# Routing of an AdaLN mixture-of-experts layer block by block instead of by pairs of blocks, with the square roots on GpSimd

## The chip, the cores and the metric

One NeuronCore of one Trainium2 chip runs the whole kernel in one launch. The metric is the device time of that launch in microseconds (us), the median of several runs; less is better. The engines are TensorE (PE, with PEld for its weight loads), VectorE (DVE), ScalarE (ACT), GpSimd (POOL) and SyncE (SP), which here only issues DMAs.

## The reference

4096 tokens (128 samples of 32) of width 256. Each sample's tokens are first mixed with a 32x32 matrix picked by the sample's condition; the result goes through a feed-forward layer with one shared part and 32 routed experts in 4 groups. Each token takes the two best groups and, in these, the eight best experts.

```
xc = einsum('bct,bcd->bdt', x, weights[conditions])
scores = sigmoid(xc @ gate_w.T)
sb = scores + gate_bias                      # (T, 32), four groups of 8
group_scores = top_k(sb by group, 2).sum()   # the best 2 of 4 groups
topi = top_k(sb of the chosen groups, 8)
w = scores[topi]; w = w / w.sum() * 2.5      # the combine weights cw
x_lat = xc @ fc1_w.T                         # width 128
h = relu(x_lat @ w1[e].T)**2 * cw[e]
routed = (sum_e h @ w2[e].T) @ fc2_w.T
shared = relu(xc @ shared_up_w.T)**2 @ shared_down_w.T
out = x + shared + routed
```

## The kernel before

The program is written by hand for each engine: five instruction lists, each executed in its own order, tied by semaphores. Nothing reorders them.

**First stage.** The tokens are 8 blocks of 512. For block b, TensorE makes `project(b)` (the condition mix, 16 matmuls), `gate_and_latent(b)` (24 matmuls, `t_banks`), and two `shared_up` units of 12 matmuls of 512 columns and two `shared_down` units of 24 matmuls of 256 columns (units 2b and 2b+1). ScalarE rounds and squares, VectorE makes the low halves (`rest`, `rest_of_projection`: every matmul is done in three terms of a high and a low part), and adds the shared result to x (`add_shared`, L946), which SP stores.

**Routing**, also in the first stage, is done on VectorE for a batch of two blocks (1024 tokens, `NB` = 8 tiles of 128 tokens, `BATCHES` = 4): `group_scores`, `pick_groups`, `largest`, `mark`, `combine_weights`. TensorE's `rank(k)` (L548 to L560) counts how many earlier tokens chose each group; VectorE reads it (`read_rank`, L1079) and makes the row index of each token in `slot_of_token`. The weight enters an expert under a square, so its square root is stored: ScalarE's `root_of_weights` (L794, a Sqrt, which needs another activation table than Sigmoid) and four VectorE operations (L1061 to L1072, a reciprocal and one Newton correction) write it into `payload`. GpSimd's `scatter(k)` (L463) then writes 16 row tiles of batch k to DRAM (`rows_dram`), two indirect DMAs for each tile of 128 tokens.

When all is counted, VectorE makes `tile_table`; SP waits for it (`table_ready`), writes four pads (L386), reads the table's entries into registers, loads the first experts' weights (L371, 8 DMAs of 512 KB), and waits for all scatters (L400) before it loads the sorted rows (`sid_sb` L359, `rows_sb` L352).

**Second stage.** 19 tiles of 512 sorted rows go through the four pairs of experts of their group, and GpSimd adds the results to the output with 76 indirect DMAs (L486). It begins on TensorE with `transpose_s(0)` (L621), which needs `sid_sb`; behind it in TensorE's list stand the last two `shared_down` units.

The experts' weights are split into high and low parts in the first stage too, group by group: SP loads the raw weights (`load_raw`, L274) only when the previous group's are split, ScalarE rounds (`round_weights`, L801), VectorE subtracts (`rest_of_weights`, L952), SP stores (`store_split`, L321).

## Time and profile before

| | |
|---|---|
| median of 3 runs | 497.52 us (496.77 to 497.75) |
| the profiled execution's own time | 494.15 us |
| its span, first to last instruction | 492.1 us |
| first stage, up to the first transpose of the second | 208.9 us |
| busy in the span: PE, DVE, ACT, POOL | 423.7, 308.4, 275.1, 204.7 us |
| instructions on POOL | 158 |
| mean granted TensorE clock | 0.927 of 2.4 GHz |

An engine's busy time says how much work it had, and not whether anything waited for it. In this kernel the first stage has gaps on every engine, and its end is set by whichever of several chains is last; the rows below are therefore mostly timelines, which give for each instruction its start, its duration and, in brackets, how long its engine had been idle and what released it.

### The profile page before, as it was taken

How to read it: one execution, taken by the hardware profiler on the slowest of the kernel's cores; microseconds unless marked ns; L12 is line 12 of the kernel's file. 1: busy time of each engine (PE TensorE's matmuls, PEld its weight loads, DVE VectorE, ACT ScalarE, POOL GpSimd, SP SyncE). 2: the span in 40 equal slices, each digit the busy share in tenths (PEclk: the TensorE clock that was granted, in tenths of full speed). 3: DMA queues.
4: the chain of work that ended last, by engine and by line, in shares of the span. 5: the costliest groups of instructions: out<-in, count | busy, mean ns of one | idle time of the engine just before them, and what ended most of it. 6: DMA issues, size and time to landing. Idle time of an engine off the chain costs nothing. (4 is left out here: it accounts for less than half of the span.)

```text
span 492.1 us, 6984 instructions
## 1 busy us (share of the span) xinstructions
PE 423.7 (86%) x2283; PEld 363.4 (74%) x2283; DVE 308.4 (63%) x494; ACT 275.1 (56%) x341; POOL 204.7 (42%) x158
## 2 busy tenths in 40 slices
PE   8798786889785996298999999999999999999940
PEld 8688685779775984286888888888888888888830
DVE  0379565097462741237887787777878778778710
ACT  1373710373434440317777777877777777777730
POOL 5010273067174076000244455554454455656554
PEclk9999985589897897789999999999999999999985
DMA  6995812715231154977689988999998999987443
GB/s 184 264 326 221 312 62 77 257 35 189 102 107 45 44 163 135 332 266 260 179 230 226 202 223 231 217 209 265 333 242 224 318 291 217 231 203 191 81 49 43
DMA packets 68125, 95.83 MB, mean 195 GB/s; under 512 B 20093, under 2 KB 49962, under 8 KB 67498
## 3 DMA queue, kind: packets, MB, share of 16 engines
q1 hardware_dynamic: 53170, 79.18, 49.6%
q0 software_dynamic: 14160, 15.87, 20.0%
q10 hardware_dynamic: 760, 0.35, 0.3%
q8 instruction: 18, 0.29, 0.2%
q14 instruction: 17, 0.14, 0.1%
HBM read 98.04 MB, written 31.00 MB: 262 GB/s over the span
## 5 line engine op out<-in xcount | busy, mean ns | idle before, releaser
L486 POOL DMA_INDIRECT out_x<-res,sid_sb x76 | 127.4, 1676 | 165.0 <-DMA out_x<-res,sid_sb 82.3
L940 DVE TENSOR_TENSOR act_lo<-act_full,act_hi 128x1024 fp32r<-128x1024 f32 x92 | 112.3, 1220 | 34.1 <-ACT act_full L790 19.3
L1149 DVE SCALAR_TENSOR_TENSOR scaled<-h_banks,cond_bd 128x1024 f32<-128x1024 f32 x76 | 92.9, 1222 | 40.0 <-PE h_banks L636 37.2
L463 POOL DMA_INDIRECT rows_dram<-payload,slot_idx x64 | 69.1, 1079 | 94.2 <-DVE payload L1072 76.0
L636 PE MATMUL h_banks<-xc_hi,w_ring 128*128 128x512 f32 x304 | 99.2, 407 | 2.2 <-issue 0.6
L657 PE MATMUL y_banks<-act_hi,w_ring 128*128 128x512 f32 x304 | 81.9, 391 | 0.8 <-ACT act_hi L811 0.8
L811 ACT ACTIVATE act_hi<-scaled 128x1024 fp32r<-128x1024 f32 x76 | 80.1, 1054 | 2.3 <-PE y_banks L657 1.6
L813 ACT ACTIVATE act_full<-scaled 128x1024 f32<-128x1024 f32 x76 | 79.9, 1051 | 0.0
L657 PEld LDWEIGHTS y_banks<-act_hi,w_ring 128*128 128x128 f32 x304 | 56.9, 188 | 13.3 <-issue 1.2
L636 PEld LDWEIGHTS h_banks<-xc_hi,w_ring 128*128 128x128 f32 x304 | 51.8, 189 | 14.9 <-issue 5.6
L636 PE MATMUL h_banks<-xc_lo,w_ring 128*128 128x512 f32 x152 | 59.6, 392 | 0.0
L595 PE MATMUL y_banks<-small_hi,act_hi 128*128 128x256 f32 x128 | 41.4, 323 | 15.4 <-issue 9.5
L657 PE MATMUL y_banks<-act_lo,w_ring 128*128 128x512 f32 x152 | 47.3, 392 | 1.6 <-DVE act_lo L940 1.6
L844 ACT ACTIVATE res<-t_banks 128x512 f32<-128x512 f32 x38 | 22.7, 598 | 43.4 <-PE t_banks L675 40.8
L595 PE MATMUL y_banks<-small_lo,act_hi 128*128 128x256 f32 x128 | 40.3, 315 | 3.7 <-issue 3.6
L781 ACT ACTIVATE scaled<-h_banks 128x1024 f32<-128x1024 f32 x16 | 16.4, 1023 | 45.6 <-remote 22.9
L595 PE MATMUL y_banks<-small_hi,act_lo 128*128 128x256 f32 x128 | 40.3, 315 | 1.6 <-issue 1.4
L595 PEld LDWEIGHTS y_banks<-small_hi,act_hi 128*128 128x128 f32 x128 | 28.5, 223 | 16.8 <-issue 12.8
L657 PEld LDWEIGHTS y_banks<-act_lo,w_ring 128*128 128x128 f32 x152 | 28.3, 188 | 8.9 <-DVE act_lo L940 2.9
L636 PEld LDWEIGHTS h_banks<-xc_lo,w_ring 128*128 128x128 f32 x152 | 28.5, 188 | 6.5
L595 PEld LDWEIGHTS y_banks<-small_hi,act_lo 128*128 128x128 f32 x128 | 28.6, 223 | 5.6 <-issue 5.4
L595 PEld LDWEIGHTS y_banks<-small_lo,act_hi 128*128 128x128 f32 x128 | 28.6, 223 | 2.9 <-issue 2.9
(131 smaller groups left out, 658.2 us busy)
## 6 DMA issues: line engine op xcount, KB each, us to landing
w_ring<-w_dram SPq DMA_DIRECT2D x76, 512.0 KB
cond_bd<-s_dram SPq DMA_DIRECT2D x76, 512.0 KB, 5.3
w_dram<-w_ring SPq DMA_DIRECT2D x8, 1024.0 KB, 8.1
rows_sb<-rows_dram SPq DMA_DIRECT2D x19, 256.0 KB
x_in<-in_x SPq DMA_DIRECT2D x8, 512.0 KB, 6.9
res<-in_experts_raw SPq DMA_DIRECT2D x4, 1024.0 KB
out_x<-x_in SPq DMA_DIRECT2D x8, 512.0 KB, 3.2
rows_dram<-in_pad_rows SPq DMA_DIRECT2D x5, 328.0 KB, 6.4
```

What stands on the lines that cost most here:

```text
L463: pool.indirect_dma_start(rows_dram, bass.IndirectOffsetOnAxis(ap=slot_idx[:, k, which, n:n + 1], axis=0), payload[:, k, n, :], None).then ...
L486: pool.indirect_dma_start(out, bass.IndirectOffsetOnAxis(ap=sid_sb[:, i % SID_RING, j, GROUP_SIZE:PER_GROUP], axis=0), res[:, i % 2, j * H ...
L595: last = pe.matmul(y_banks[:, j * H:(j + 1) * H], v, w, start=slot == 0 and j % 2 == 0 and n == 0, stop=slot == 1 and j % 2 == 1 and n == ...
L636: last = pe.matmul(h_banks[:, s, m * BANK:(m + 1) * BANK], w, v, start=n == 0, stop=n == 2)
L657: last = pe.matmul(y, w, v, start=u == 0 and n == 0 and m == 0, stop=u == PAIRS - 1 and n == 2 and m == 1)
L781: act.activation(scaled[:, u % 2, :], h_banks[:, slot_of["u", u], :], ACT.Relu).then_inc(relu_ready, 1)
L811: act.activation(act_hi[:, u % 2, :], scaled[:, u % 2, :], ACT.Square).then_inc(act_hi_ready, 1)
L813: act.activation(act_full[:, u % 2, :], scaled[:, u % 2, :], ACT.Square).then_inc(act_full_ready, 1)
L844: act.activation(res[:, i % 2, part * BANK:(part + 1) * BANK], t_banks[:, 1, :], ACT.Copy)\
L940: dve.tensor_tensor(act_lo[:, s, :], act_full[:, s, :], act_hi[:, s, :].bitcast(f32), ALU.subtract).then_inc(act_lo_ready, 1)
L1149: dve.scalar_tensor_tensor(scaled[:, u % 2, :], h_banks[:, slot_of["e", n], :], 0.0, scale_ring[:, u, :], ALU.max, ALU.mult).then_inc(scal ...
```

## The change

- A routing batch is now one block: `BATCHES` = 8, `NB` = 4. Every routing operation is issued twice as often on half as many elements. The batch's scatter is 8 indirect DMAs.
- ScalarE's Sqrt, VectorE's reciprocal and correction, the clamp and the mask of nonzero weights go away. `roots(k)` on GpSimd clamps the weight, makes a first guess of the inverse root by integer arithmetic on its bits, improves it by three Newton steps of four operations, and multiplies by the weight: 16 operations of 128x128 elements, each waiting for the one before through `root_step`.
- GpSimd's list is now `roots(k)`, `scatter(k)` for k = 0 to 7.
- The scores have a ring of four blocks, the combine weights a ring of two: VectorE's `combine_weights(k)` waits for `roots(k-2)`.
- The first stage's lists of TensorE, ScalarE, VectorE and SP are written in a new order. `rank(k)` now waits also for the last `gate_and_latent` to have been read.

```diff
-BATCHES = BLOCKS // 2
-NB = 2 * BT
+BATCHES = BLOCKS
+NB = BT
+SCORES_RING = 4
+CW_RING = 2
...
+            def step(instruction):
+                instruction.then_inc(root_step, 1)
+                steps[0] += 1
+                pool.wait_ge(root_step, steps[0])
+
+            def roots(k):
+
+                pool.wait_ge(cw_ready, k + 1)
+                weight = cw[:, k % CW_RING, :, :]
+                step(pool.tensor_scalar(clamped[:, :, :], weight, TINY, None, ALU.max))
+                step(pool.tensor_scalar(root[:, :, :].bitcast(i32), clamped[:, :, :].bitcast(i32), -0.5, INVERSE_ROOT,
+                                        ALU.mult, ALU.add))
+                for _ in range(ROOT_STEPS):
+                    step(pool.tensor_tensor(squared[:, :, :], root[:, :, :], root[:, :, :], ALU.mult))
+                    step(pool.tensor_tensor(squared[:, :, :], squared[:, :, :], clamped[:, :, :], ALU.mult))
+                    step(pool.tensor_scalar(squared[:, :, :], squared[:, :, :], -0.5, 1.5, ALU.mult, ALU.add))
+                    step(pool.tensor_tensor(root[:, :, :], root[:, :, :], squared[:, :, :], ALU.mult))
+
+                step(pool.tensor_scalar(squared[:, :, :], weight, 0.0, None, ALU.max))
...
+                pool.tensor_tensor(dst[:, :, :, 0:GROUP_SIZE], by_group(squared[:, :, :]), by_group(root[:, :, :]),
+                                   ALU.mult).then_inc(s_ready, 1)
...
-            scatter(0)
-            scatter(1)
-            scatter(2)
-            scatter(3)
+            for k in range(BATCHES):
+                roots(k)
+                scatter(k)
...
             gate_and_latent(2)
+            shared_up(2)
             gate_and_latent(3)
-            shared_up(2)
             shared_up(3)
+            rank(1)
             project(4)
...
+            rank(7)
+            count_all()
+            shared_down(10)
+            shared_up(12)
...
-            def root_of_weights(k):
-                act.wait_ge(cw_ready, k + 1)
-                act.activation(root[:, :, :], masked[:, :, :], ACT.Sqrt, scale=0.25).then_inc(root_ready, 1)
...
-            rest_of_weights(0)
             group_scores(0)
+            pick_groups(0)
+            largest()
+            mark()
+            combine_weights(0)
             rest(0)
-            pick_groups(0)
+            group_scores(1)
             rest(1)
             rest_of_projection(2)
...
+            combine_weights(1)
+            rest_of_weights(0)
+            group_scores(2)
...
+            combine_weights(7)
+            rest(9)
+            add_shared(4)
             rest(10)
-            combine_weights(3)
-            add_shared(4)
-            read_rank(3)
-            slot_of_token(3)
-            root_of_weights(3)
+            read_rank(7)
+            slot_of_token(7)
+            tile_table()
             rest(11)
-            tile_table()
```

GpSimd's list, the place after the ids are written, before the change (one batch; three more like it follow):

```order
L463 DMA rows_dram<-payload,slot_idx 18944x164 [waits s_ready,idx_ready,lat_copied,ids_ready]
L463 DMA rows_dram<-payload,slot_idx 18944x164 x15
L463 DMA rows_dram<-payload,slot_idx 18944x164 [waits s_ready,idx_ready,lat_copied,ids_ready]
L463 DMA rows_dram<-payload,slot_idx 18944x164 x15
```

The same place after the change (the middle Newton steps are left out here; seven more batches follow):

```order
L473 TENSOR_SCALAR s_t<-s_t 128x128 [waits cw_ready]
L474 TENSOR_SCALAR s_t<-s_t 128x128 [waits root_step]
L477 TENSOR_TENSOR s_t<-s_t 128x128 [waits root_step]
L478 TENSOR_TENSOR s_t<-s_t 128x128 [waits root_step]
L479 TENSOR_SCALAR s_t<-s_t 128x128 [waits root_step]
L480 TENSOR_TENSOR s_t<-s_t 128x128 [waits root_step]
...
L482 TENSOR_SCALAR s_t<-s_t 128x128 [waits root_step]
L488 TENSOR_TENSOR payload<-s_t 128x4x4x8 [waits root_step]
L498 DMA rows_dram<-payload,slot_idx 18944x164 [waits s_ready,idx_ready,lat_copied,ids_ready]
L498 DMA rows_dram<-payload,slot_idx 18944x164 x7
```

Between two runs of scatters GpSimd now has 16 operations of its own, one behind the other.

VectorE's list, first batch, before the change: the end of `mark`, a projection's rest, and `combine_weights` (rows_sb holds the routing's scratch, s_t the weights).

```order
L1041 MATCH_REPLACE rows_sb<-top,rows_sb 128x32 x7
L932 TENSOR_TENSOR xc_lo<-h_banks,xc_hi 128x1024 [waits xc_hi_ready,gate_step]
L1045 SCALAR_TENSOR_TENSOR rows_sb<-rows_sb,scores 128x256
L1048 TENSOR_REDUCE total<-rows_sb 128x8 [waits gate_step]
L1050 RECIPROCAL total<-total 128x8 [waits gate_step]
L1052 SCALAR_TENSOR_TENSOR s_t<-rows_sb,total 128x256 [waits gate_step]
L1056 TENSOR_SCALAR rows_sb<-s_t 128x256 [waits gate_step]
L1057 TENSOR_SCALAR s_t<-s_t 128x256
```

The same place after the change:

```order
L1084 MATCH_REPLACE rows_sb<-top,rows_sb 128x32 x3
L1088 SCALAR_TENSOR_TENSOR rows_sb<-rows_sb,scores 128x128 [waits gate_step]
L1091 TENSOR_REDUCE total<-rows_sb 128x4 [waits gate_step]
L1093 RECIPROCAL total<-total 128x4 [waits gate_step]
L1098 SCALAR_TENSOR_TENSOR s_t<-rows_sb,total 128x128 [waits gate_step]
L983 TENSOR_TENSOR act_lo<-act_full,act_hi 128x1024 [waits act_full_ready,act_hi_ready]
```

The first block's weights are now complete ahead of the first `rest`, on half the elements, and two operations of `combine_weights` are gone.

## Rows read from the trace of the kernel before

**Rows 1.** Busy time by stretch of the span, core 0

```profile
core 0: us, PE busy (x) PEld busy (x) DVE busy (x) ACT busy (x) POOL busy (x), PEclk, DMA share, GB/s
58.00:100.00 42.00, 30.22 (x159) 27.80 (x158) 20.37 (x66) 12.51 (x16) 16.45 (x16) 0.72 0.39 138
100.00:200.00 100.00, 83.03 (x483) 73.93 (x481) 53.54 (x162) 40.30 (x44) 52.62 (x48) 0.88 0.34 111
209.00:492.00 283.00, 260.05 (x1283) 214.26 (x1283) 203.62 (x191) 193.24 (x247) 127.38 (x76) 0.96 0.84 214
```

**Rows 2.** Timeline of TensorE: start us, duration us

```profile
208.91 0.40 PE L621 MATMUL t_banks<-ident,sid_sb 128*36 128x128 f32 x1 [8.79 <-DMA sid_sb<-rows_dram]
```

**Rows 3.** Timeline of the DMAs that SP issues

```profile
20.56 0.51 SPq L299 DMA_DIRECT2D bias_sb<-in_gate_b  x1
...
176.36 5.06 SPq L386 DMA_DIRECT2D rows_dram<-in_pad_rows  x4
191.27 6.44 SPq L371 DMA_DIRECT2D w_ring<-w_dram  x8
...
201.26 0.70 SPq L359 DMA_DIRECT2D sid_sb<-rows_dram  x1
```

**Rows 4.** Timeline of GpSimd, the last scatter

```profile
193.11 0.97 POOL L463 DMA_INDIRECT rows_dram<-payload,slot_idx  x1 [0.31 <-issue]
```

**Rows 5.** Groups of GpSimd's instructions: busy us, mean ns | idle before

```profile
L463 POOL DMA_INDIRECT rows_dram<-payload,slot_idx x64 | 69.1, 1079 | 94.2 <-DVE payload L1072 76.0 <-issue 18.3
L452 POOL COPY payload<-ids_sb 128x32 int32<-128x32 int32 x4 | 2.1, 596 | 20.3 <-DMA consts_sb<-in_table_consts 20.3
...
L434 POOL TENSOR_SCALAR_AFFINE_SELECT ident<-ident 128x128 f32<-128x128 f32 x1 | 0.3, 286 | 0.2 <-POOL tri L432 0.2
L432 POOL MEMSET tri<- 128x128 f32 x1 | 0.2, 212 | 0.0
```

**Rows 6.** GpSimd's instructions on the payload tile: duration ns min/median/max

```profile
L452 POOL COPY payload<-ids_sb x4: 240/454/1235, 28.7 to 30.5; 128x32 int32<-128x32 int32 x4
```

**Rows 7.** Timeline of VectorE, the first batch's routing

```profile
30.09 0.42 DVE L979 TENSOR_TENSOR rows_sb<-scores,bias_sb 128x256 f32<-128x256 f32 x1
...
33.46 1.23 DVE L940 TENSOR_TENSOR act_lo<-act_full,act_hi 128x1024 fp32r<-128x1024 f32 x1
34.60 0.28 DVE L1004 TENSOR_TENSOR group_gt<-group_score 128x128 f32<-128x128 f32 x1
...
36.88 1.23 DVE L940 TENSOR_TENSOR act_lo<-act_full,act_hi 128x1024 fp32r<-128x1024 f32 x1
...
39.16 0.83 DVE L1036 MAX8 top<-rows_sb 128x8 f32<-128x32 f32 x8
...
41.44 1.23 DVE L932 TENSOR_TENSOR xc_lo<-h_banks,xc_hi 128x1024 fp32r<-128x1024 f32 x1
42.58 0.41 DVE L1045 SCALAR_TENSOR_TENSOR rows_sb<-rows_sb,scores 128x256 f32<-128x256 f32 x1
...
44.18 0.29 DVE L1056 TENSOR_SCALAR rows_sb<-s_t 128x256 f32<-128x256 f32 x1
```

**Rows 8.** Groups of VectorE's instructions, 20 to 200 us

```profile
L979 DVE TENSOR_TENSOR rows_sb<-scores,bias_sb 128x256 f32<-128x256 f32 x4 | 1.7, 421 | 2.2 <-ACT scores L772 2.2
L1005 DVE TENSOR_TENSOR group_eq<-group_score 128x128 f32<-128x128 f32 x4 | 1.1, 284 | 0.0
```

**Rows 9.** DMA issues: KB each, median us from issue to landing

```profile
out_x<-x_in SPq DMA_DIRECT2D x8, 512.0 KB, 3.2
sid_sb<-rows_dram SPq DMA_DIRECT2D x19, 18.0 KB, 4.5
bias_sb<-in_gate_b SPq DMA_DIRECT2D x1, 16.0 KB, 7.7
```

**Rows 10.** Waits up to 230 us: us in total, times, longest

```profile
ACT scaled L781 <- remote: 22.9, 3, 11.4
PE y_banks L595 <- issue: 14.5, 16, 3.0
```

More of the change, by code:

```diff
@@ L885, in _ @@
             square_shared(7)
-            latent_and_scores(6)
+            round_weights(3)
             latent_and_scores(7)
@@ L1044, in combine_weights @@
             def combine_weights(k):
-                step(dve.scalar_tensor_tensor(work[:, :, :], left[:, :, :], TAKEN, scores[:, k % 2, :, :],
+                step(dve.scalar_tensor_tensor(work[:, :, :], left[:, :, :], TAKEN, scores[:, k % SCORES_RING, :, :],
                                               ALU.is_equal, ALU.mult))
@@ L1188, in _ @@
             mark()
+            combine_weights(2)
             rest_of_projection(5)
[L1190 to L1191 removed]
+            read_rank(2)
+            slot_of_token(2)
             add_shared(1)
[L1193 to L1200 removed]
+            group_scores(3)
+            pick_groups(3)
@@ L1217, in _ @@
+            rest(4)
+            pick_groups(4)
+            read_rank(3)
+            slot_of_token(3)
+            rest(5)
+            rest_of_projection(6)
             largest()
             mark()
-            rest(10)
-            combine_weights(3)
-            add_shared(4)
-            read_rank(3)
-            slot_of_token(3)
-            root_of_weights(3)
+            combine_weights(4)
+            group_scores(5)
+            rest(6)
+            add_shared(2)
+            pick_groups(5)
@@ new lines, in _ @@
+            largest()
+            mark()
+            combine_weights(5)
+            rest_of_weights(2)
+            rest_of_projection(7)
+            read_rank(4)
+            slot_of_token(4)
+            group_scores(6)
+            rest(7)
+            pick_groups(6)
+            read_rank(5)
+            slot_of_token(5)
+            largest()
+            mark()
+            combine_weights(6)
+            add_shared(3)
+            rest_of_weights(3)
+            group_scores(7)
+            rest(8)
@@ L1225, in _ @@
+            pick_groups(7)
+            read_rank(6)
+            slot_of_token(6)
+            largest()
+            mark()
+            combine_weights(7)
+            rest(9)
+            add_shared(4)
+            rest(10)
+            read_rank(7)
+            slot_of_token(7)
+            tile_table()
             rest(11)
-            tile_table()
             add_shared(5)
```

170 lines of the change are left out of this document (74 added, 96 removed).

## The prediction

> **What bounds the kernel now.** I read first the busy time by stretch. From 209 us on TensorE is busy for 260 of 283 us [rows 1]: the second stage is full, no line of it is changed, and I take its 492.1 - 208.9 = 283.2 us as fixed. Before it, between 58 and 200 us, TensorE is busy for 30.2 + 83.0 = 113 of 142 us and VectorE for 74, the granted clock being 0.72 and 0.88 of 2.4 GHz [rows 1]. So the first stage has holes, and what counts is what ends last in it.
>
> The timelines show that. The second stage begins at 208.91 us, after TensorE sat idle for 8.79 us for the landing of `sid_sb` [rows 2]. SP issued that load at 201.26 [rows 3]. It could not do so sooner, as all scatters must have landed, and GpSimd issued the last of them at 193.11, done at 194.1 [rows 4]. Both landings were slow: 7 us for the scatter (194.1 to 201.2) and 7.6 for the load, where such a load takes 4.5 at the median and a store like it 3.2 [rows 9]. The reader should look at what lies beside them: SP had issued 4 MB of expert weights from 191.27 to 197.7 [rows 3]. So three chains meet at the end of the stage: GpSimd's scatters (194.1); SP's table chain (the table is read from about 175.3 just ahead of the first pad, the pads go out at 176.4, the registers are read, the weights go out from 191.3 to 197.7, some 22.4 us in all) [rows 3]; and TensorE's own work.
>
> GpSimd is the engine to watch. It sat idle for 76.0 us for the payload [rows 5]; one scatter DMA costs 1.079 us busy and 18.3/60 = 0.305 us of issue [rows 5], 1.384 together, so 64 of them need 88.6 us.
>
> **The change, part by part.** *The first batch is ready sooner.* On VectorE the batch of two blocks took 3.37 us for the group scores (30.09 to 33.46), 2.28 for the choice of groups (34.60 to 36.88), 2.28 for `largest` and `mark` (39.16 to 41.44), and 1.60 for the part of `combine_weights` that stays (42.58 to 44.18) [rows 7]. A 256-element operation takes 0.421 us, a 128-element one 0.284 [rows 8], so each of the full-size ones loses 0.137: six in the scores, one in the choice, three in the combination. For the 128-element operations that become 64 I take half of that, 0.07, five times. `largest` and `mark` halve. That gives 2.5 + 1.8 + 1.15 + 1.2 = 6.65 us for one block. It starts when the bias has landed, 20.56 + 7.7 = 28.3 us [rows 3, 9]; the first block's scores are there by then, and in VectorE's new list nothing stands between. So the first weights are ready at 28.3 + 6.65 = 35.0 us, where GpSimd's first scatter of before had waited for two whole blocks and for ScalarE's root.
>
> *GpSimd's roots.* 16 operations of 128x128, six with one input and ten with two. The profile has no row of such a two-input operation. One-input: 0.286 us [rows 5], I take 0.30. Two-input: bounded below by the same 0.286 and above by the copy of 0.454 at the median, on strided data [rows 6]; I take 0.38, between them. Each operation waits for the one before. The handover is bounded below by nothing and above by the 0.2 us that GpSimd idled for its own memset [rows 5]; I take 0.10. That makes 6 x 0.40 + 10 x 0.48 = 7.2 us. Then there is VectorE. One of the four id copies took 1.235 us against a median of 0.454 [rows 6], while VectorE worked on the experts' weights with operations of 1.2 us. The mean was 0.596 [rows 5], 0.142 more than the median. On 16 operations that is 2.3 us; VectorE is busy for about half of this stretch and for 2/3 of it where work is dense [rows 1], so I take 1.5. Sum: **8.7 us a block**, with bounds of 16 x 0.212 = 3.4 (a memset of that size [rows 5]) and 16 x (0.454 + 0.2) = 10.5, plus contention.
>
> The Trainium skill (GPSIMD Engine Reference, Elementwise — side-by-side cycle accounting) gives GpSimd about 2.6 cycles an element for two inputs, and advises VectorE for such work. By its figures a two-input operation would be about 0.34 us, an estimate from that page, and the roots 6.3 to 6.8 us before contention. The same notes (SBUF — State Buffer, SBUF: two separate sides) state that a GpSimd operation and a VectorE operation with two SBUF inputs lock each other out of a shared port for a whole instruction. The copy of 1.235 us agrees with it.
>
> *GpSimd's whole chain.* A block's scatter is 8 x 1.384 = 11.1 us, so a block costs 19.8 us, and eight of them 158.4. From 35.0 us on, less the issue gap behind the last DMA (about 0.4), it ends at **193.0 us**, against 194.1. GpSimd is never starved after that start if each block's weights come every 19.8 us: VectorE's routing is about 6.65 + 0.9 us a block, 60 us in all, and GpSimd needs block 7 at 35.0 + 7 x 19.8 = 173.6 us only. So nearly all that the early start and the removed waits win, the roots consume, 8 x 8.7 = 70 us of it.
>
> *What stands ahead of the second stage.* Here is the gain that I expect. If the last weights load is through when the last scatter lands, that landing takes 3.2 us and the load of `sid_sb` 4.5 [rows 9], with 0.2 for SP: 193.0 + 3.2 + 0.2 + 4.5 = 200.9 us for the first transpose, 8.0 us sooner than 208.9. It asks that SP's table chain of 22.4 us plus the time of the 4 MB has ended by about 193, so that the table is ready at some 165 us instead of 175. In the new lists rank(7) stands two and a half units later in TensorE's shared work than rank(3) did, but every routing step ahead of it is shorter, `tile_table` goes ahead of rest(11), and the gaps of TensorE between 58 and 200 us (29 us of idle time, and a clock at 1.2 GHz for part of it) are the reserve.
>
> *Work moved or removed off the path.* ScalarE loses four Sqrts and the table loads around them, VectorE a reciprocal of 256 elements per batch; both engines are under 60% busy there [rows 1], so I count nothing, and if that cover were gone it would be a microsecond or two per batch in favour. TensorE gains four matmul instructions. The split of the experts' weights comes later in VectorE's list; ScalarE's next `round_weights` then waits for a load behind that, and `round_projection(4)` and `(6)` are queued behind it, so TensorE's up and down units wait some microseconds twice. GpSimd's chain hides it as long as it has 20 us in hand at block 5 and later; without that cover it costs perhaps 10 us. `combine_weights(k)` waits for `roots(k-2)`: behind it on VectorE are the rests that TensorE waits for. That too only binds when GpSimd is last anyway.
>
> *Sum.* 494.15 - 8.0 = 486.2 us for a profiled execution. The median stands 3.4 us above the profiled time, so **489.5 us**.
>
> **The rivals.** *GpSimd dearer (slower).* The place is `roots(k)`, L473 to L488. Each microsecond more per block costs 8 us at the end, as nothing refills the chain. It decides at 8.7 + 1.0 = 9.7 us a block: above it the stage ends later than 208.9. At 10.5 us, the upper bound without contention, the end is 489.5 + 8 x 1.8 = 504 us; with the full contention more. For it: no measured two-input row, and 16 handovers. Against it: the one-input row is short. Chance 0.25.
>
> *GpSimd cheaper.* At 6.3 us a block the chain ends at 173.8 us and is no longer last. Then TensorE's own stage is. Its 113 us of busy work after 58 us with some waits would end about 185 to 190, and its first transpose then needs no wait: 497.5 - (208.9 - 187) = 476 us. Chance 0.2.
>
> *The table chain stays late (no change).* TensorE is held up in a strange way: 14.5 us for nothing that the profile names, up to 3.0 at once, and ScalarE got its signal late three times, 22.9 us in all [rows 10]. These fall into GpSimd's runs of 16 scatters, mostly their second half. If runs of 8 with a pause bring as much, the table is again ready at 175 or later, the weights collide with the last landings, and all is as before: 495 to 499 us. For it: the DMAs are as many. Against it: the second stage scatters in runs of four and shows little of it. Chance 0.13.
>
> **How the numbers follow.** Forecast (GpSimd's chain last, roots of 7.7 to 9.6 us): 0.42, 481 to 497 us, nearly all of it faster. Cheaper roots: 0.2, 473 to 481. Late table: 0.13, 494 to 500. Dearer roots: 0.25, 498 to 512. The 8 in 10 range, with the lowest and the highest tenth left out, is 476 to 505 us. A difference of 0.2%, 1 us, is about what a measurement tells from none. Faster by more: 0.40 + 0.2 + 0.05 = 0.65; within it 0.08; slower 0.27.
>
> **What would show it.** Right: on GpSimd's timeline, blocks of roots and scatters back to back from about 55 us, a first root near 35 us, 8 to 9.5 us per 16 operations, idle time for the payload gone, and the last scatter at about 192 us; the load of `sid_sb` landing in 4 to 5 us; TensorE's idle time before the first transpose still there, ended by the DMA. Wrong: GpSimd idle for `cw_ready` or `idx_ready` after 60 us (then VectorE or TensorE bounds), the weights load issued after 188 us, or operations of 0.5 us and more.

## The result, and the profile after

The changed kernel takes **495.11 us** (median of 20 runs), the kernel before 495.66 us (median of 20) in the same comparison. The ratio is 1.0096, 95% interval 1.0065 to 1.0128: **slower by 1.0%**, where I forecast 489.5 us and faster. Ratios, here and below, leave out executions more than 1.5% above the fastest of their kernel, while medians count them all, and by the medians the two kernels are level. The profiled execution took 492.43 us, its span is 490.4.

The kernel before has two levels, about 495 us in some comparisons and about 468 in others. Within one comparison it keeps its level, and one chip has shown both. The changed kernel takes 493 to 495 us at either level.

| comparison | before | changed | ratio |
|---|---|---|---|
| the first | 495.66 | 495.11 | 1.0096 |
| experiments, set 1 | 467.62 | 493.4 | 1.0551 [1.0506, 1.0596] |
| set 3 | 494.81 | 493.5 | 0.9996 [0.9958, 1.0034] |

First the busy time of the changed kernel by stretch, to be laid beside [rows 1] (columns as there).

```profile
58.00:100.00 42.00, 37.66 (x260) 35.37 (x260) 27.20 (x106) 17.78 (x21) 33.19 (x51) 0.92 0.49 168
100.00:200.00 100.00, 69.75 (x406) 63.39 (x405) 52.68 (x188) 33.75 (x37) 79.43 (x114) 0.82 0.46 161
```

TensorE does 7.4 us more before 100 us than before, at a clock of 0.92 instead of 0.72, and 13.3 us less behind it. GpSimd is busy for 113 of 142 us instead of 69. Then the timelines of TensorE, of SP's DMAs and of GpSimd, which answer to [rows 2 to 4].

```profile
206.78 0.40 PE L663 MATMUL t_banks<-ident,sid_sb 128*36 128x128 f32 x1 [19.69 <-DMA sid_sb<-rows_dram]
```

```profile
169.56 5.08 SPq L392 DMA_DIRECT2D rows_dram<-in_pad_rows  x4
181.88 4.71 SPq L377 DMA_DIRECT2D w_ring<-w_dram  x8
...
204.30 0.70 SPq L365 DMA_DIRECT2D sid_sb<-rows_dram  x1
```

```profile
201.70 0.96 POOL L498 DMA_INDIRECT rows_dram<-payload,slot_idx  x1 [0.30 <-issue]
```

The last scatter is issued 8.6 us later than in [rows 4]. TensorE had nothing to do for 19.69 us, since 187.1. The table was read some 7 us sooner (pads at 169.56, [rows 3] has 176.36), so the weights are through by 186.6 and the two landings behind the last scatter are short: from its end at 202.66 to the load 1.6 us, and 2.5 us more to the transpose. So the second stage starts 2.1 us sooner than in [rows 2], and takes 490.4 - 206.8 = 283.6 us. The last view is GpSimd's groups (busy, mean ns | idle before), for [rows 5].

```profile
L498 POOL DMA_INDIRECT rows_dram<-payload,slot_idx x64 | 67.1, 1049 | 24.1 <-issue 17.1 <-POOL payload L488 6.2 <-ACT payload L819 0.9
L478 POOL TENSOR_TENSOR s_t<-s_t 128x128 f32<-128x128 f32 x24 | 15.1, 629 | 1.9
L480 POOL TENSOR_TENSOR s_t<-s_t 128x128 f32<-128x128 f32 x24 | 12.1, 503 | 2.0
L477 POOL TENSOR_TENSOR s_t<-s_t 128x128 f32<-128x128 f32 x24 | 9.9, 414 | 1.9
L479 POOL TENSOR_SCALAR s_t<-s_t 128x128 f32<-128x128 f32 x24 | 9.4, 390 | 2.1
L473 POOL TENSOR_SCALAR s_t<-s_t 128x128 f32<-128x128 f32 x8 | 6.0, 744 | 5.5 <-DVE s_t L1098 5.0
L482 POOL TENSOR_SCALAR s_t<-s_t 128x128 f32<-128x128 f32 x8 | 5.3, 659 | 0.7
L488 POOL TENSOR_TENSOR payload<-s_t 128x128 f32<-128x128 f32 x8 | 5.0, 624 | 0.7
L474 POOL TENSOR_SCALAR s_t<-s_t 128x128 int32<-128x128 int32 x8 | 3.9, 487 | 0.7
```

The roots are busy for 66.7 us, 8.3 a block. Here are rows of the fifth block, at a time when VectorE has only short operations (0.08 to 0.47 us). Just before them L473, at 118.80, had taken 1.54 us instead of 0.53, beside a `rest` of 1.23 us on VectorE that had begun at 118.73.

```profile
120.43 0.30 POOL L474 TENSOR_SCALAR s_t<-s_t 128x128 int32<-128x128 int32 x1
120.82 0.40 POOL L477 TENSOR_TENSOR s_t<-s_t 128x128 f32<-128x128 f32 x1
121.29 0.46 POOL L478 TENSOR_TENSOR s_t<-s_t 128x128 f32<-128x128 f32 x1
121.84 0.30 POOL L479 TENSOR_SCALAR s_t<-s_t 128x128 f32<-128x128 f32 x1
...
126.69 0.53 POOL L482 TENSOR_SCALAR s_t<-s_t 128x128 f32<-128x128 f32 x1
```

Between two of them lie some 0.08 us, and 0.87 to 0.97 between the last one and the first scatter (6.2 us for seven blocks). So a block's roots cost 8.3 + 1.2 + 0.9 = 10.4 us. The idle time for the payload, 76.0 us in [rows 5], is gone: from the first root at 34.4 us on GpSimd has no gap longer than that step into a block's first scatter.

### The profile page after: what moved, and what is told of

Read it like the earlier page. It is cut to its first block and busy times, and to the rows that moved or that the text cites. A ratio compares the mean times of both kernels' runs of the same rounds, so it can differ in the third digit from the quotient of the medians.

```text
span 490.4 us, 7262 instructions
## 1 busy us (share of the span) xinstructions
PE 417.9 (85%) x2291; PEld 360.5 (74%) x2291; DVE 316.1 (64%) x594; ACT 267.2 (54%) x332; POOL 265.8 (54%) x290
## 5 line engine op out<-in xcount | busy, mean ns | idle before, releaser
L520 POOL DMA_INDIRECT out_x<-res,sid_sb x76 | 124.5, 1638 | 157.7 <-DMA out_x<-res,sid_sb 76.6
L498 POOL DMA_INDIRECT rows_dram<-payload,slot_idx x64 | 67.1, 1049 | 24.1 <-issue 17.1
L637 PE MATMUL y_banks<-small_hi,act_hi 128*128 128x256 f32 x128 | 39.6, 309 | 8.7 <-DVE act_lo L983 6.4
L833 ACT ACTIVATE scaled<-h_banks 128x1024 f32<-128x1024 f32 x16 | 16.4, 1025 | 49.9 <-PE h_banks L619 34.4
L637 PE MATMUL y_banks<-small_hi,act_lo 128*128 128x256 f32 x128 | 38.6, 302 | 0.0
L637 PE MATMUL y_banks<-small_lo,act_hi 128*128 128x256 f32 x128 | 38.6, 301 | 0.0
L637 PEld LDWEIGHTS y_banks<-small_hi,act_hi 128*128 128x128 f32 x128 | 27.1, 212 | 10.0 <-issue 7.0
L678 PEld LDWEIGHTS h_banks<-xc_lo,w_ring 128*128 128x128 f32 x152 | 28.5, 188 | 6.5
L575 PE MATMUL t_banks<-small_hi,xc_hi 128*128 128x160 f32 x64 | 19.7, 308 | 10.1 <-DVE rank_at L1106 8.1
L619 PE MATMUL h_banks<-xc_hi,small_hi 128*128 128x512 f32 x64 | 27.7, 432 | 0.0
```

Source lines behind the costliest of these rows:

```text
L498: pool.indirect_dma_start(rows_dram, bass.IndirectOffsetOnAxis(ap=slot_idx[:, k, which, n:n + 1], axis=0), payload[:, k, n, :], None).then ...
L520: pool.indirect_dma_start(out, bass.IndirectOffsetOnAxis(ap=sid_sb[:, i % SID_RING, j, GROUP_SIZE:PER_GROUP], axis=0), res[:, i % 2, j * H ...
L575: last = pe.matmul(gf_tiles[:, j // 2, j % 2, :], v, w, start=n == 0, stop=n == len(terms) - 1)
L619: last = pe.matmul(h_banks[:, s, m * BANK:(m + 1) * BANK], w, v, start=n == 0, stop=n == len(terms) - 1)
L637: last = pe.matmul(y_banks[:, j * H:(j + 1) * H], v, w, start=slot == 0 and j % 2 == 0 and n == 0, stop=slot == 1 and j % 2 == 1 and n == ...
L678: last = pe.matmul(h_banks[:, s, m * BANK:(m + 1) * BANK], w, v, start=n == 0, stop=n == 2)
```

## Experiments

Each was timed in five rounds. In brackets stands the ratio to the kernel before in the same comparison with its 95% interval.

### Set 1: what the roots cost, and who should make them (before: 467.62 us)

**The changed kernel again.**

> The changed kernel once more, for the ratio on this chip and a second profile. Theory A (GpSimd's chain of roots and scatters ends the first stage): ratio to the kernel before 0.995 to 1.012; on the profile GpSimd works without a gap from about 35 us to about 202 us, one block every 21 us, and the first transpose of the second stage starts some 4 us after it ends. Rival B (the halved batches and the new lists on VectorE and TensorE cost the time): the last shared unit on TensorE would end later than GpSimd's last scatter in some profile; in the first it ended at 187 us against 202.7.

493.4 us [1.0506 to 1.0596]; first transpose at 205.52, last scatter at 200.51. The trace is as theory A had it, but the ratio is 1.0551 instead of 0.995 to 1.012. The changed kernel had not moved; the kernel before was 28 us faster than in the first comparison.

**Two Newton steps instead of three** (coarser roots).

```
-ROOT_STEPS = 3
+ROOT_STEPS = 2
```

> Two Newton steps in place of three (four GpSimd operations fewer per block, 0.40 + 0.46 + 0.30 + 0.46 us and 4 x 0.08 of handover, 1.95 us without contention). Theory A: the chain ends 8 x 2 = 16 us sooner, at about 186 us, where TensorE's own stage (187 us) takes over, so the time falls by 14 to 17 us against the changed kernel, ratio to it 0.966 to 0.972. Rival B: no more than 2 us.

485.64 us [1.0331 to 1.0449], 7.8 less than the changed kernel: half of the 14 to 17 that theory A gave, and more than rival B's 2. The last scatter was issued 16.3 us sooner (184.22 against 200.51), as expected. But SP issued the 4 MB of weights from 179.45 to 184.2, right ahead of its landing. The load of `sid_sb` was issued only 12.4 us sooner (190.67 against 203.10) and took 6.1 us to land, and the second stage was 3 us longer. So GpSimd's chain was last, and 4 operations a block are worth 8 us in the end, about half of what they take.

**The roots on VectorE**, the same operations, right behind `combine_weights`.

```
             for k in range(BATCHES):
-                roots(k)
                 scatter(k)
...
             combine_weights(0)
+            roots(0)
```

> All else as changed, but the same 16 operations per block stand on VectorE, right behind combine_weights; GpSimd only scatters. About 16 x 0.31 = 5 us per block more in VectorE's list, 40 us in all, in front of the rests that TensorE waits for. Theory A: GpSimd's chain is 8 x 10.7 = 85 us long and no longer last; the first stage then ends with TensorE and VectorE, between 190 and 200 us instead of 206.8, so 7 to 17 us faster than the changed kernel. Rival B (VectorE and TensorE set the end already): slower than the changed kernel by 10 us or more, as VectorE gets 40 us more.

513.56 us [1.091 to 1.1013]: 20 us slower than on GpSimd. The waits of TensorE up to its second stage (us, times, longest):

```profile
PE t_banks L552 <- DVE rank_at L1110: 14.3, 2, 10.0
PE y_banks L614 <- DVE act_lo L960: 12.4, 2, 7.0
```

TensorE waits for VectorE's routing and rests; its first transpose comes at 225.58. Moving the roots off VectorE was right for these lists, though GpSimd is slow.

**The kernel before with nothing but the roots moved to GpSimd**: its batches of 1024 and its lists stay.

```
-            scatter(0)
-            scatter(1)
-            scatter(2)
-            scatter(3)
+            for k in range(BATCHES):
+                roots(k)
+                scatter(k)
```

> One part of the change alone: the kernel before with its lists and its batches of two blocks, the roots made by GpSimd as in the change (16 operations of 128x256, about 0.7 us each, some 12 us a batch), ScalarE's Sqrt and VectorE's correction gone. Theory A: in this order the batches come late (GpSimd idled 76 us), so the roots fill idle time in batches 0 to 2, but the last batch's 12 us stand between its weights (163 us) and its scatter, which then starts at 176 instead of 171.6 us: 3 to 6 us slower than the kernel before. Rival B: GpSimd's roots are hidden altogether and the time is that of before within 1 us, or lower because the table loads are gone.

478.66 us [1.0193 to 1.0282]: 11 us slower than before and 15 us faster than the changed kernel. TensorE was done with the first stage at 190.66 - 35.07 = 155.6 us here, against 187.1 with the new lists. So the new lists, with the small blocks, cost TensorE some 30 us, and the roots on GpSimd hide that. GpSimd's chain could have been what held TensorE up there, by way of VectorE's wait for `roots(k-2)`. The trace of the changed kernel has that wait once, for 2.5 us (`DVE s_t L1098 <- POOL payload L488`), so that it is not the 30 us.

### Set 2: where does the kernel before lose 28 us? (before: 497.99 us)

**The kernel before, profiled again.**

> The kernel before, unchanged, profiled on this chip. In the comparison in which the changed kernel was 1% faster it took 490 to 504 us, in the first experiments 465 to 471, while the changed kernel took 492 to 494 in both. Theory (the time moved in the first stage, by stalls in which no engine of the chip's records has work): where it takes about 467, the second stage from the first transpose on takes 283 to 287 us as ever, the first transpose comes at 181 to 185 instead of 208.9, and the gaps of about 1 us marked issue between GpSimd's scatters are gone. Rival (the clock): the granted clock is higher all through, and both stages are shorter in proportion, the second by 8 us or more.

503.39 us, and a profile (of an execution of 502.51 us) like the first: first transpose at 213.87. TensorE's gaps of over 0.25 us that are marked issue, from 30 to 190 us, sum to 16.6 us (17 of them); in the trace of [rows 10] to 17.3 (16).

**No Newton step** (the first guess is the root).

> The changed kernel with no Newton step: the roots are the first guess only, so that the values of the weights are coarser; 12 of the 16 GpSimd operations of a block's roots are left out. Theory (GpSimd's chain is last, and behind it the new lists' TensorE work, which ended at 187 in the changed kernel): the chain stops being the last at once, the first transpose comes when TensorE and the table are ready, at 185 to 190, and the time is 472 to 478, no less although the GpSimd work is 50 us shorter. Rival (GpSimd's traffic slows the other engines, and all would end sooner without it): 455 to 465.

487.52 us [0.9801 to 0.9915], 10 above the theory's range and 22 above the rival's. The last scatter is issued at 173.81, 28 us sooner than in the changed kernel, and yet the transpose waits for TensorE's work until 191.8 and for the DMA until 197.39. So with GpSimd's roots nearly gone the new lists hold the first stage to about 190. 10.8 us of it are issue gaps. 8.5 of these are two single gaps (3.88 and 4.63 us); as the changed kernel has one of 5.6 at the 468 level too (at 144.8 us in its trace of set 1), how much of them is stall stays open.

**The changed kernel's lists and blocks with the old roots** (ScalarE's Sqrt, five VectorE operations, GpSimd only scatters).

```
+            def root_of_weights(k):
+                act.wait_ge(cw_ready, k + 1)
+                act.activation(root[:, :, :], clamped[:, :, :], ACT.Sqrt, scale=0.25).then_inc(root_ready, 1)
```

> The changed kernel's blocks of 512 tokens and lists, with the roots as the kernel before makes them: ScalarE's square root and five VectorE operations for each block, GpSimd only scatters. Theory (the new lists hold TensorE's first stage to about 187, whoever makes the roots, because VectorE's routing stands in front of what TensorE waits for): VectorE gets some 2 us more per block, TensorE's last unit of the first stage ends at 190 to 200, the time is 475 to 490. Rival (only the roots on GpSimd cost time, and routing by blocks is good by itself): 465 or less, at or below the kernel before on this chip.

504.23 us [1.0121 to 1.0236]. Slower than the theory's 475 to 490, but this comparison was at the 495 level. With no roots between them, two blocks' scatters ran into each other as 16 in a row (131.4 to 151.8 us), with three issue gaps of 1.0 to 1.1 us at the end. The number without stalls follows in set 4.

**The kernel before with GpSimd's roots of two steps.**

> The kernel before with its lists and its batches of 1024 tokens, the roots alone made on GpSimd, with two Newton steps instead of three (coarser roots). With three steps GpSimd's chain ended last, 35 us after TensorE's work. Theory (chain last, and each step is four operations of about 0.55 us at 256 elements, so 2.2 us a batch): 8 to 10 us less than with three steps, about 469, which is level with the kernel before on the chip of the first experiments. Rival (another thing holds the chain, such as the indices or VectorE's weights): less than 4 us gained.

496.85 us [0.9971 to 1.0058]: 18 us *slower* than the same kernel with three steps in set 1. Neither theory has that, and it was the key. (The trace of the kernel with two steps is of a long execution, 509.03 us; the kernel before shows the same in one of 494.15, in set 5.) Two traces of nearly the same program can be laid side by side. First TensorE in the kernel with three steps, at the 468 level (same stretch as below):

```profile
66.72 0.28 PE L625 MATMUL y_banks<-small_hi,act_hi 128*128 128x256 f32 x1
...
66.96 0.28 PE L625 MATMUL y_banks<-small_lo,act_hi 128*128 128x256 f32 x1
67.08 0.28 PE L625 MATMUL y_banks<-small_hi,act_hi 128*128 128x256 f32 x1
67.20 0.28 PE L625 MATMUL y_banks<-small_hi,act_lo 128*128 128x256 f32 x1
```

and in the kernel with two, at the 495 level:

```profile
66.74 0.28 PE L625 MATMUL y_banks<-small_hi,act_hi 128*128 128x256 f32 x1
67.06 0.28 PE L625 MATMUL y_banks<-small_hi,act_lo 128*128 128x256 f32 x1
...
69.95 0.37 PE L625 MATMUL y_banks<-small_hi,act_hi 128*128 128x256 f32 x1 [0.46 <-issue]
71.38 0.37 PE L625 MATMUL y_banks<-small_hi,act_lo 128*128 128x256 f32 x1 [1.06 <-issue]
72.82 0.37 PE L625 MATMUL y_banks<-small_lo,act_hi 128*128 128x256 f32 x1 [1.07 <-issue]
```

Up to 66.7 us the same matmuls start within 0.02 us of each other. Then one kernel goes on with a matmul every 0.12 us, and the other slows to one every 0.7 us and soon to one every 1.4, until about 79.9 us. Nothing that a matmul waits for is missing: they are in the middle of one unit. GpSimd was in a run of 16 scatters, one every 1.27 us, that ended at 77.4.

### Set 3: are the long runs of scatters the cause? (before: 494.81 us)

**A pause in the middle of each run of 16.**

```
                 for n in range(NB):
+                    if n == NB // 2:
+                        for _ in range(PAUSE):          # 24
+                            pauses[0] += 1
+                            pool.memset(spare[:, :], 0.0).then_inc(pause_step, 1)
+                            pool.wait_ge(pause_step, pauses[0])
```

> The kernel before, with a pause after the first 8 of a batch's 16 scatters: 24 memsets on GpSimd, one after the other, about 7 us. Theory (TensorE's instructions come late when more than some 6 scatters are issued without a break, on the chips where the kernel before takes about 495): on such a chip the rows marked issue in TensorE's first stage shrink from 17 us to under 5, TensorE's first stage ends 10 to 25 us sooner, GpSimd's end comes later by at most the 7 us of the last batch, and the time is 470 to 487 against 495. On a chip where the kernel before takes about 467 it costs 0 to 7 us. Rival (the stalls come from something else in the kernel before, such as VectorE's or ScalarE's order): 495 to 502, and the issue rows stay.

483.07 us [0.9736 to 0.986]: **10 us faster by the ratio, 12 by the medians, by doing nothing for 6.3 us four times**. The issue gaps fall from 17 to 8.2 us, and not under 5 as the theory had it. The trace shows why: the second 8 of the second batch ran without a break into the first 8 of the third (16 scatters from 109.65 to 129.9 us), and right behind them TensorE has gaps of 0.82 and 1.15 us and ScalarE a wait of 12.2 us that the profile marks remote, that is, for which it names no instruction that released it.

**A wait after every 4 scatters until all have landed.**

```
                     for which in range(TOP_GROUPS):
+                        issued = 2 * (NB * k + n) + which
+                        if issued % GROUP == 0 and issued > 0:          # GROUP = 4
+                            pool.wait_ge(rows_scattered, DMA * issued)
```

> The kernel before, with GpSimd waiting after every 4 scatters until all have landed. Theory (a backlog of scatters stalls TensorE's issue): with at most 4 outstanding no issue rows are left; each wait costs GpSimd a landing of 2 to 3 us, so a batch's 16 scatters take about 28 us instead of 20, and the last ends 8 us later or is hidden; time 475 to 490 on a chip where the kernel before takes about 495. Rival (it is the number of scatters issued, not what is outstanding): the issue rows stay at 10 us or more, 495 to 505.

477.93 us [0.957 to 0.9706]: **3.6% below the kernel before and 3.2% below the changed one**. The wait in GpSimd's timeline, and TensorE's waits up to the first transpose:

```profile
62.92 0.97 POOL L467 DMA_INDIRECT rows_dram<-payload,slot_idx  x1 [0.30 <-issue]
65.78 0.97 POOL L467 DMA_INDIRECT rows_dram<-payload,slot_idx  x1 [1.88 <-DMA rows_dram<-payload,slot_idx]
```

```profile
PE t_banks L625 <- DMA sid_sb<-rows_dram: 24.1, 1, 24.1
PE y_banks L599 <- issue: 6.1, 3, 3.0
```

6.1 us of issue is near the floor (the kernel before and its versions with waits have 4.8 to 6.8 at the 468 level, set 4 and 5), and no wait is marked remote any more. TensorE is done at 165.8 us; now the last batch's scatters, stretched by three waits, are last (184.7).

**Runs of 16 in the changed kernel**: two blocks' roots, then two blocks' scatters.

```
-            for k in range(BATCHES):
+            for k in range(0, BATCHES, 2):
                 roots(k)
+                roots(k + 1)
                 scatter(k)
+                scatter(k + 1)
```

> The changed kernel, with the roots of two blocks made first and then the scatters of both, 16 in a row as in the kernel before; GpSimd's work is the same. Theory (runs of 16 bring the stalls back on the chips that have them): issue rows of 10 us or more in TensorE's first stage instead of 1 to 6, and 497 to 510 against 493 to 495. On a chip without them, and by the rival (the run's length does not matter): 492 to 497, since GpSimd's chain is last either way.

504.34 us [1.003 to 1.0182]. Its ratio, 1.0106, is 1.1% or 5 us above that of the changed kernel beside it (0.9996), its median 10.8 us; even its lowest time, 496.83, is above the highest of the changed kernel, 496.45. The trace is of one of its long executions (512.01 us), so the sizes in it are not those of the median. In it the last scatter is issued at 199.75, no later, but TensorE's first stage ends at 217.1 instead of 191.3. The issue gaps are 17.0 us, 7.8 of it one gap, against 8.0 beside it. The stall is back in TensorE's timeline, from the ninth scatter of the second run on:

```profile
119.86 0.37 PE L555 MATMUL h_banks<-cond_bd,x_in 128*128 128x128 f32 x1 [1.88 <-issue]
121.27 0.37 PE L555 MATMUL h_banks<-cond_bd,x_in 128*128 128x128 f32 x1 [1.04 <-issue]
122.68 0.57 PE L555 MATMUL h_banks<-cond_bd,x_in 128*128 128x128 f32 x1 [1.04 <-issue]
```

**The changed kernel beside them.**

> The changed kernel once more, on the chip of this set. Theory: it takes 492 to 496 on every chip, whatever the kernel before takes there (467 or 495), since its scatters come 8 at a time. Rival (the chips differ in something that every kernel feels): the changed kernel moves with the kernel before, by a third of its difference or more.

493.5 us [0.9958 to 1.0034], the same number as at the 468 level. So the change made the kernel's time nearly immune to the stalls. Its trace is not free of them. Waits up to 200 us (us, times, longest):

```profile
ACT payload L819 <- remote: 13.4, 2, 9.5
DVE x_in L989 <- remote: 10.2, 1, 10.2
```

At the 468 level the same kernel has none. These waits, and one more of 4.6 us, end 1.3 to 1.7 us behind the end of a run of 8 scatters each (at 57.17, 78.17, 138.77 and 180.73 us). They cost nothing here, as GpSimd's chain ends the first stage and issues its last scatter at 200.64, where it was 200.51 without them. So the immunity has two parts: shorter runs, and a longer chain on GpSimd that hides what is left.

### Set 4: the changes alone, without stalls (before: 467.60 us)

**Waits after every 4 or every 8 scatters, but not in the last batch** (the condition gets `and k < BATCHES - 1`, and `GROUP` is 4 or 8).

> The kernel before, with GpSimd waiting after every 4 scatters until all have landed, but not within the last batch, behind whose scatters only the second stage waits. Theory (with waits throughout, the last batch's scatters took from 155.8 to 185.7, of which the three waits between them are about 10 us, and TensorE had been done for 24 us): the last scatter ends 8 to 10 us sooner and the time is 466 to 471 on any chip. Rival (the stalls come back in the last batch's run of 16 and hold TensorE there): 477 or more.

> The same with the wait after every 8 scatters instead of 4. Theory (stalls begin after some 7 or 8 scatters in a row, and the changed kernel's runs of 8 are nearly free of them): 466 to 474, within 1% of the waits after every 4. Rival (8 outstanding are already too many): issue rows of over 10 us in TensorE's first stage, 480 or more.

468.77 us [1.0012 to 1.0061] and 467.11 us [0.9968 to 1.0031]. Both are in their expected range, but this comparison was at the 468 level, where nothing is to be won. It shows that the waits cost next to nothing there (0.4% after every 4, nothing after every 8).

**The changed lists and blocks, old roots, waits after every 4.**

> The changed kernel's lists and blocks of 512, the roots made by ScalarE and VectorE as before, and GpSimd waiting after every 4 scatters until all have landed. It took 504 without the waits on a chip with stalls. Theory (the lists and the small blocks cost by themselves, because VectorE has more instructions and TensorE waits for it): TensorE's first stage ends at 180 to 195 where the kernel before's ends at about 165, time 480 to 492. Rival (the lists are as good as the old ones, all of it was stalls and roots): 472 or less.

490.25 us [1.0439 to 1.0539], 21.5 more than the kernel before with waits after every 4 but in the last batch, beside it. TensorE's waits up to its second stage:

```profile
PE t_banks L571 <- ACT scores L805: 12.9, 3, 9.4
PE t_banks L644 <- DMA sid_sb<-rows_dram: 9.8, 1, 9.8
PE y_banks L618 <- issue: 6.6, 1, 6.6
PE t_banks L556 <- DVE rank_at L1123: 4.3, 2, 3.5
```

Its first stage ends at 201.60 - 9.82 = 191.8 us, with the old lists and batches at 162.4. Theory right: the lists and blocks cost by themselves, whoever makes the roots. My version of ScalarE's places for the roots is one of several, so that the size is an upper bound for the lists alone.

**The changed kernel with waits after every 4.**

> The changed kernel, with GpSimd waiting after every 4 scatters until all have landed; nothing else changed. Theory (GpSimd's chain is last, and a wait in the middle of each block's 8 scatters lengthens it by 1.7 to 2.3 us, eight times, while the one behind them is mostly covered by the roots): the last scatter ends at 215 to 222 and the time is 504 to 512. Rival (its own stalls, 1 to 8 us in its profiles, hold it): 490 or less.

517.4 us [1.1048 to 1.1132]. Its last scatter ends at 222.8, just above the range of 215 to 222, and the time is 5 us above its own. It has no issue gap over 0.25 us at all, so stalls of its own don't hold the changed kernel; GpSimd's chain does: its last scatter came 21.3 us later than in the trace of set 1, and the time is 24.0 us longer.

### Set 5: what depends on the comparison (before: 468.04 us)

> The kernel before, unchanged. Theory: where it takes 465 to 471, its first stage has issue rows of under 5 us in sum and its first transpose comes at 180 to 185; where it takes 490 or more, issue rows of 12 to 20 us and a first transpose at 205 to 215. Rival (the chips differ in another way, in the clock or the DMA): the issue rows are the same in sum on both kinds of chip, and the second stage is shorter on the fast ones by more than 5 us.

467.87 us [0.9972 to 1.0036]: the profile that was missing. TensorE, SP, a wait of GpSimd up to 178 us, and the busy time by stretch:

```profile
179.11 0.40 PE L621 MATMUL t_banks<-ident,sid_sb 128*36 128x128 f32 x1 [15.69 <-DMA sid_sb<-rows_dram]
```

```profile
149.60 5.11 SPq L386 DMA_DIRECT2D rows_dram<-in_pad_rows  x4
```

```profile
POOL rows_dram L463 <- DVE payload L1072: 47.8, 4, 27.5
```

```profile
58.00:100.00 42.00, 34.67 (x223) 32.49 (x223) 31.70 (x113) 20.45 (x24) 25.36 (x23) 0.88 0.44 152
```

The same program, 29.8 us sooner at the first transpose than in [rows 2]. Pads at 149.6 instead of 176.36 [rows 3], 47.8 us of waiting for the payload instead of 76.0 [rows 5], a clock of 0.88 instead of 0.72 [rows 1]; issue gaps 6.8 us instead of 17.3 (the theory had said under 5, and a transpose at 180 to 185). The second stage is not shorter (466.0 - 179.1 = 286.9 us against 283.2), so the rival of a faster clock or DMA all through falls. Where it begins can be seen to the matmul. The kernel before at the 495 level, in the middle of a down unit:

```profile
71.62 0.28 PE L595 MATMUL y_banks<-small_hi,act_hi 128*128 128x256 f32 x1
71.74 0.28 PE L595 MATMUL y_banks<-small_hi,act_lo 128*128 128x256 f32 x1
72.84 0.28 PE L595 MATMUL y_banks<-small_lo,act_hi 128*128 128x256 f32 x1 [0.82 <-issue]
74.24 0.28 PE L595 MATMUL y_banks<-small_hi,act_hi 128*128 128x256 f32 x1 [1.12 <-issue]
```

and at the 468 level:

```profile
71.64 0.28 PE L595 MATMUL y_banks<-small_lo,act_hi 128*128 128x256 f32 x1
71.76 0.28 PE L595 MATMUL y_banks<-small_hi,act_hi 128*128 128x256 f32 x1
71.88 0.28 PE L595 MATMUL y_banks<-small_hi,act_lo 128*128 128x256 f32 x1
72.00 0.28 PE L595 MATMUL y_banks<-small_lo,act_hi 128*128 128x256 f32 x1
```

GpSimd's scatters start at 58.27 and 58.33 us and go on alike. From the eleventh on (71.94 us) TensorE gets an instruction every 0.7 to 1.4 us. The direct loss is 10 us of issue, and ScalarE and VectorE wait 41.8 us for signals marked remote where they have no such wait at the 468 level; the rest is what follows. The granted clock falls to 0.50 while TensorE has little to do and stays there up to 84 us, and each later batch starts later: the second run of scatters by 11.9 us (101.46 against 89.55), the third by 17.4, the last by 26.0 (171.57 against 145.55).

The waits marked remote tell the levels apart better than the issue gaps do. Here are both, summed for each trace (issue: TensorE's gaps of over 0.25 us from 30 to 190 us; remote: all engines, from 30 to 200 us):

| trace | scatters in a row | issue, us | remote, us |
|---|---|---|---|
| 495 level: kernel before (first comparison, set 2) | 16 | 17.3, 16.6 | 41.8, 35.0 |
| its roots on GpSimd, two steps | 16 | 23.5 | 36.2 |
| with a pause after 8 | 8, once 16 | 8.2 | 54.7 |
| with waits after every 4 | 4 | 6.1 | 0 |
| changed kernel (first comparison, set 3) | 8 | 0.8, 8.0 | 8.2, 28.2 |
| no Newton step | 8 | 10.8 | 28.5 |
| changed lists, old roots | 8, once 16 | 9.7 | 46.2 |
| changed kernel, runs of 16 | 16 | 17.0 | 61.0 |
| 468 level: all ten traces | 4 to 16 | 0 to 9.2 | 0 |

So runs of 8 shorten the issue gaps, but other engines still get signals late behind them; only with waits after every 4 was there nothing left of it.

> The kernel before with GpSimd waiting after every 8 scatters until all have landed, but not within the last batch. Theory (the stalls need longer runs than 8): 465 to 472 on any chip, that is 4 to 6% below the kernel before where that takes about 495, and level with it where it takes about 467. Rival (the chips differ in something that every kernel feels): 485 or more where the kernel before takes about 495.

468.36 us [0.9955 to 1.0024], again at the 468 level. So the best version (waits after every 8 but in the last batch) is level with the kernel before where that is fast and 5% below the changed kernel; at the 495 level it has not been run, and since the traces with 8 in a row have 8 to 55 us of remote waits there, it is open whether 8 would be few enough. There the waits after every 4 gave 477.9, of which those in the last batch are about 9 us, an estimate from its first transpose (189.90) and that of the kernel without them in the last batch at the 468 level (180.53).

## Why the prediction was wrong

**The step that failed is the cost of GpSimd's roots, 8.7 us a block; it is 10.4.** The mechanism (GpSimd's chain is last, nothing refills it) was right, the size was not, and I had put the turning point at 9.7.

| term | predicted | measured |
|---|---|---|
| 16 operations, undisturbed | 6 x 0.30 + 10 x 0.38 = 5.6 | 6.7 |
| handovers | 16 x 0.10 = 1.6 | 15 x 0.08 = 1.2 |
| contention | 1.5 | 8.3 - 6.7 = 1.6 |
| last operation to first scatter | 0 | 0.9 |
| roots of a block | 8.7 | 10.4 |
| 8 scatters and their issue | 11.1 | 10.7 |
| block | 19.8 | 21.1 |

An undisturbed two-input operation takes 0.40 (L477) or 0.46 us (L478, L480), not 0.38, and the two `max` operations, which I had counted as one-input, 0.53 instead of 0.30. The bound that I took from a strided copy (0.454) was the better value. The Trainium skill (GPSIMD Engine Reference, Elementwise — side-by-side cycle accounting) led, by its figures, to an estimate of about 0.34 us; the trace disagrees, 0.40 to 0.46. And I had no term at all for the 0.9 us between the last operation and the first scatter, which waits on four semaphores (behind the memsets of before_pause, with one, it was 0.28).

Point by point: the first weights came at 34.4 us (predicted 35.0). The chain was never starved behind its first root, as said. Its end came at 202.7 instead of 193.0: 8 x 1.3 - 0.6. The landings behind it were cheaper than I took from the medians, 4.1 us instead of 7.9, which gave 3.8 back; that the median came as near to the forecast as 5.6 us is owed to this. So the first transpose came at 206.8 (200.9). The second stage took 283.6 (283.2). Profile 492.4 (486.2), median 495.1 (489.5).

**The rivals.** The dearer roots were the one that happened, at 10.4 us a block and 495 us, where I had worked out 504 at 10.5, since it did not have the shorter landings. The table chain did not stay late: the table was ready some 7 us sooner, and TensorE's part ended at 187 as I had estimated (185 to 190).

**What the range could not hold is the other side of the comparison.** I took the time of before as a property of its program. It is not: the first trace was of an execution with stalls. I had seen them, 14.5 us for nothing that the profile names and 22.9 us of late signals [rows 10], and had made it a rival that runs of 8 bring as much of it. They bring less: that is the real gain of the change. Runs of 16 put back into the changed kernel cost 5 us by the ratios and 10.8 by the medians, and the pause and the waits in the kernel before win 12 and 17 us. The gain goes back into GpSimd's roots and into lists and blocks that let TensorE's first stage end at 187 us instead of 163. Without stalls nothing is won and 26 us are lost: 205.5 against 179.1 us at the first transpose, 493.4 against 467.6 in time. With them the two kernels are level within 1%.

**Open.** What makes a comparison one of the stalled kind isn't settled; the same chip gave both levels. Nor is it why a run of scatters slows the issue of another engine's instructions: the runs show when it comes (behind the eighth to eleventh scatter of a run where it is strong, and some runs of 16 in the same traces have next to none of it), not the mechanism. The number of scatters in a row and the number still outstanding were not told apart either: the pause and the waits lower both. And the lists and the small blocks were not tried apart.

## What to carry to other kernels

A cost that the profile can't name ("issue", "remote") on an engine in the middle of independent work is a lead, not noise: look at what another engine was issuing at the time, and break that up first, as it costs three lines. An engine that waits is a good place to put work only as long as its whole chain, counted with each handover and the step into its first DMA, ends before the others; here 8 x 10.4 = 83 us on GpSimd took more than its 76 us of slack, and without the stalls the slack is only 47.8. And when a reordering is judged, profile the kernel before again in the comparison that decides: here its level alone moved the ratio between 1.00 and 1.055.

## What the hardware showed

- **A long run of GpSimd's indirect DMAs can slow TensorE's instruction issue and delay other engines.** In the stalled comparisons a matmul was issued every 0.7 to 1.4 us instead of every 0.12, from the eighth to eleventh scatter of a run (one every 1.27 us) up to 3 us behind its end, and ScalarE and VectorE had 35 to 61 us of waits marked remote in traces with runs of 16, 8 to 29 in those with runs of 8 alone. Waiting for the landing after every 4 ended both. Pauses of 6.3 us after 8 halved the issue gaps and left the remote waits. In other comparisons, on the same chip too, neither occurred.
- **The first scatter behind the last root operation**, with waits on four semaphores between them, starts 0.87 to 0.97 us after it; behind a memset and one wait 0.28; the next ones 0.30 after each other.
- **GpSimd's elementwise operations on 128x128 float32**, undisturbed: 0.30 us for multiply-add with constants, 0.40 and 0.46 for two inputs, 0.53 for `max`; beside a busy VectorE 1.6 us at worst, and 0.63 on average for L478.
